# A Perceiver block in fp32: the first attention's value projection by seven products of matrix quarters, its bias behind the weighing, queries and the results' high parts through DRAM

## The reference

```
q = query @ Wq + bq                      # 16 x 64 x 1024, 16 heads of 64
k = key @ Wk + bk                        # 16 x 512 x 1024
v = value @ Wv + bv                      # 16 x 512 x 1024, key = value = ctx_1024
attn = softmax(einsum('bqhd,bkhd->bhqk', q, k) / 8)
out = einsum('bhqk,bkhd->bqhd', attn, v) @ Wo + bo + residual
```

## Time and profile before

| | us |
|---|---|
| median of the runs | 1711.32 |
| the profiled execution | 1711.51 |
| its span, first to last instruction | 1709.7 |
| PE busy | 1615.2 |
| DVE busy | 1163.9 |
| ACT busy | 938.0 |
| POOL busy | 307.3 |

### The profile page before, as it was taken

How to read it: one execution, slowest core, us unless ns; L and a number is a source line. 1 busy time by engine, 2 the same in 40 slices (tenths; PEclk the granted TensorE clock), 3 DMA queues, 4 the chain that set the end, 5 groups by cost and what they waited for, 6 DMA issues and landing times. The chain is left out here.

```text
span 1709.7 us, 27478 instructions
## 1 busy us (share of the span) xinstructions
PE 1615.2 (94%) x10730; PEld 1361.0 (80%) x10730; DVE 1163.9 (68%) x1978; ACT 938.0 (55%) x1700; POOL 307.3 (18%) x258
## 2 busy tenths in 40 slices
PE   7999999999999999999999878994899999999987
PEld 6888888888888888888887766773788888888876
DVE  4277777877777777777777666775768448548842
ACT  5466666666666666666666433442656336336631
POOL 4201211011101110111100161565311011101101
PEclk9999999999999999999999999996999999999899
DMA  6601830111101110111002560114757437528711
GB/s 228 212 24 54 131 77 7 54 57 54 37 27 53 57 54 8 54 56 54 7 5 80 173 187 14 55 57 138 249 150 212 141 87 242 155 89 247 221 39 21
DMA packets 54107, 165.21 MB, mean 97 GB/s; under 512 B 10612, under 2 KB 10996, under 8 KB 53408
## 3 DMA queue, kind: packets, MB, share of 16 engines
q1 hardware_dynamic: 38032, 131.88, 22.6%
q0 software_dynamic: 15920, 31.19, 8.7%
HBM read 143.54 MB, written 55.64 MB: 117 GB/s over the span
## 5 line engine op out<-in xcount | busy, mean ns | idle before, releaser
L413 PE MATMUL psum<-ctx,Wk 128*128 128x512 f32 x1536 | 386.2, 400 | 0.0
L413 PE MATMUL psum<-Wv,ctx 128*128 128x512 f32 x1536 | 368.7, 389 | 0.0
L413 PEld LDWEIGHTS psum<-Wv,ctx 128*128 128x128 f32 x1536 | 288.3, 188 | 59.9
L413 PEld LDWEIGHTS psum<-ctx,Wk 128*128 128x128 f32 x1536 | 280.1, 189 | 55.9
L932 DVE SCALAR_TENSOR_TENSOR kT<-psum,bkc,kT 64x512 fp32r<-64x512 f32 x256 | 191.9, 750 | 170.0 <-ACT kT L1322 165.8
L413 PE MATMUL psum<-xgT,Wh 128*128 128x224 f32 (+5 forms) x1536 | 250.0, 316 | 15.1 <-issue 10.2
L413 PEld LDWEIGHTS psum<-xgT,Wh 128*128 128x128 f32 x1536 | 228.4, 196 | 32.7 <-issue 12.6
L766 PE MATMUL psum<-Wh,hs 128*128 128x512 f32 x981 | 245.6, 396 | 0.0
L1332 ACT ACTIVATE Pr<-Pr,smn 128x512 f32<-128x512 f32 x128 | 92.6, 724 | 233.9 <-DVE smn L941 233.9
L1322 ACT ACTIVATE kT<-psum,bkc 64x512 fp32r<-64x512 f32 x256 | 175.1, 684 | 77.7 <-PE psum L413 73.8
L766 PEld LDWEIGHTS psum<-Wh,hs 128*128 128x128 f32 x981 | 181.1, 190 | 33.7 <-DVE hs L1207 0.3
(11 more groups left out here) (154 smaller groups left out, 1911.1 us busy)
## 6 DMA issues: line engine op xcount, KB each, us to landing
raw<-in_W SPq DMA_DIRECT2D x128, 512.0 KB, 4.3
expert_rows<-in_spare_rows SPq DMA_DIRECT2D x16, 1042.0 KB, 7.3
raw<-in_ctxT SPq DMA_DIRECT2D x32, 512.0 KB, 4.4
xg<-expert_rows POOLq DMA_DIRECT2D x32, 256.0 KB, 5.9
low_parts<-Olo POOLq DMA_DIRECT2D x32, 128.0 KB, 2.4
oT<-low_parts SPq DMA_DIRECT2D x8, 512.0 KB, 4.3
out_x<-x SPq DMA_DIRECT2D x12, 256.0 KB, 2.2
xs<-in_x SPq DMA_DIRECT2D x4, 512.0 KB, 6.8
```

Source lines behind the costliest of these rows:

```text
L413: mm = pe.matmul(dst, l, r, start=n == 0, stop=n == len(pairs) - 1)
```

## The change

**Seven products.** Context (512 keys by 512) and Wv (512 by 1024) are cut in quarters, A11 to A22 and B11 to B22. Four sums of context quarters (S1 to S4) and four of weight quarters (T1 to T4) are made, and the values come from seven quarter products, where eight tiles' worth of products stood: P1 = A11 B11, P2 = A12 B21, P3 = S4 B22, P4 = A22 T4, P5 = S1 T1, P6 = S2 T2, P7 = S3 T3. A product covers one tile of 128 keys and 512 dims and has 6 matmuls. For each batch there are two groups G = 2b + p of seven products (84 matmuls, 96 before). The order in the steps is fixed by `v_products(n)`: P1 and P6 in steps j = 2 and 6, P2 and P7 in j = 3 and 7, P4 and P5 in j = 4 and 0, P3 alone in j = 5 and 1. PE does `weigh` ahead of them now. `weigh` waits until both groups of its batch are done. Two PSUM banks serve the products in turn.

**Moving them out.** ACT copies P1 to a value tile (`move_v`); DVE adds the others to tiles, one addition each for P6, P2, P7, P4 and P3, and two for P5 (`evict_v`). That is 12 additions on DVE per batch for 8.

**Sums.** Per batch POOL makes four sums of 128x512 (`ctx_sums`) and four low parts (`sums_low`), ACT four high parts (`sums_high`, at the end of steps 4, 4, 6 and 7). For batch 0 DVE does POOL's part behind the last query product. The sums of weights are made once, on DVE and ACT, while queries are projected.

**Bias.** bv is added to the weighed result: `o_high` and `o_low` are now four instructions of 64 columns each, since the bias differs from head pair to head pair.

**DRAM.** Each query tile goes to `q_rows` in DRAM through a ring of four (`qst`, POOL's DMA) and comes back batch by batch (`qb`). The queries qs are built for half a batch at a time, in steps 2 and 6. The results' high parts go to `high_parts` beside the low ones, and SP fetches both before the output products.

**Elsewhere.** `d_gate(NT - 1)`, ACT's exponential in the routing of the last tile, stands ahead of the high part of the fourth expert weight tile. In the experts DVE's `weighted` waits for all chunks (`y_psum`) where it began at the first (`y_ready`), and POOL issues small DMAs for the missing chunks for every expert.

The diff, cut to its core:

```diff
+        V_ORDER = ("P1", "P6", "P2", "P7", "P4", "P5", "P3")
+        def v_bank(G, name):
+            return bank[2 + (7 * G + V_ORDER.index(name)) % 2]
+        def v_products(n):
+            if n < 2:
+                return ((0, "P1"), (0, "P6")) if n == 0 else ((0, "P2"), (0, "P7"), (0, "P4"), (0, "P5"))
+            G, names = {2: ((n + 2) // 4, ("P1", "P6")), 3: ((n + 1) // 4, ("P2", "P7")), 0: (n // 4, ("P4", "P5")), 1: ((n - 1) // 4, ("P3",))}[n % 4]
+            return (((0, "P3"),) if n == 2 else ()) + (tuple((G, name) for name in names) if G < NG else ())
...
@@ tensor_program: weigh
-                pe.wait_ge(v_done, HALF * (u + 1))
+                b, g = divmod(u, 2)
+                pe.wait_ge(v_done, 7 * (2 * b + 2))
...
-            for n in range(HALF):
-                project_v(n)
             for n in range(NS + 3):
                 if n < NS:
                     project_k(n)
                 if 0 <= n - 1 < NS:
                     scores(n - 1)
-                if n + HALF < NS:
-                    project_v(n + HALF)
                 if n >= 6 and n % HALF == 2:
                     weigh(n // HALF - 1)
+                for G, name in v_products(n):
+                    project_v(G, name)
                 if 0 <= n - 2 < NS:
                     turn(n - 2)
@@ vector_program
+            def evict_v(G, name):
+                n, src = 7 * G, v_bank(G, name)
+                v.wait_ge(v_psum, n + V_ORDER.index(name) + 1)
+                if name == "P6":
+                    v.wait_ge(v_moved, G + 1)
...
+                elif name == "P5":
+                    v.wait_ge(v_done, n + 4)
+                    v.tensor_tensor(v_tile(G, 1, 1), src, v_tile(G, 1, 1), ALU.add).then_inc(v_done, 1)
+                    v.tensor_tensor(v_tile(G, 0, 1), src, v_tile(G, 0, 1), ALU.add).then_inc(v_done, 1)
@@ scalar_program
+                for s_ in range(HALF):
+                    high = s.activation(Ohr[u % 4][:, s_, :], bank[7][:, s_ * TB:(s_ + 1) * TB], ACT.Identity,
+                                        bias=bvc[:, HALF * half + s_:HALF * half + s_ + 1])
...
-                if n < NS and j == 2 and b + 1 < B:
-                    build_qbd(b + 1)
+                for G, name in v_products(n):
+                    move_v(G, name)
+                if n % HALF == 2 and n // HALF + 1 < NS // HALF:
+                    build_qbd(n // HALF + 1)
...
+                if n < NS and b + 1 < B and j in (4, 6, 7):
+                    sums_high(b + 1, {4: ("S2", "S3"), 6: ("S1",), 7: ("S4",)}[j])
...
-            split_first(3)
             d_gate(NT - 1)
+            split_first(3)
@@ gpsimd_program
+            for n in range(2 * NJ):
+                g.wait_ge(q_done, n + 1)
+                g.dma_start(q_rows[n // NJ, n % NJ], qst[n % 4][:]).then_inc(q_out[n % 4], 16)
...
+                if b < B:
+                    ctx_sums(b)
...
+                    sums_low(b)
```

More of the change, by code:

```diff
@@ L243, in perceiver_block @@
         y_psum, y_ready, y_done, out_added, scattered = (sem(n) for n in ("y_psum", "y_ready", "y_done", "out_added", "scattered"))
-        out_wide = [sem(f"out_wide{q}") for q in range(2 * E)]
+        out_wide = sem("out_wide")
         LAG = 3
@@ L299, in sync_program, with fetch_qb @@
             fetch_ctx(0)
[L300 to L304, removed]
+            for k in range(KD):
+                fetch(L_WK + k, a["Wk"][k * P:(k + 1) * P, :])
+            for m, k in enumerate(VK):
+                fetch(L_WV + m, a["Wv"][k * P:(k + 1) * P, :])
+            for c in range(2):
+                fetch(sum_load(0, c), a["ctxT"][0, :, 2 * c:2 * c + 2, :])
+            def fetch_qb(b):
+                half, at = divmod(b, 8)
+                if b < 2:
+                    for r in range(4):
+                        sp.wait_ge(q_out[r], 64 if r <= b else 32)
+                else:
+                    sp.wait_ge(qbd_hi, 8 * (b - 1))
+                    sp.wait_ge(qbd_lo, 4 * (b - 1))
+                if b == 8:
+                    for r in range(4):
+                        sp.wait_ge(q_out[r], 64)
+                sp.dma_start(qb[b % 2][:], q_rows[half, :, :, at * TB:(at + 1) * TB].rearrange("j p t -> p j t")).then_inc(qb_in[b % 2], 16)
+            fetch_qb(0)
+            fetch_qb(1)
             for b in range(B):
@@ L472, in tensor_program, with key_tile @@
                 project_q(n, slice(n // NJ * 512, n // NJ * 512 + 512), True)
[L474 to L488, removed]
-                else:
-                    pe.wait_ge(v_done, n - 1)
-                products(v_bank(n), split_pairs([pair(ctx[b % 2], slice(None), k, ks) for k in range(KD)],
-                                                      [pair(Wv, slice(None), k, cs) for k in range(KD)])).then_inc(v_psum, 1)
+            def key_tile(x, p):
+                return [[x[i][:, kk, p * P:(p + 1) * P] for i in range(2)] for kk in range(2)]
@@ L553, in c_product @@
                     pe.wait_ge(o_lo, NS // HALF)
-                products(c_bank(t), split_pairs([(Ohi[:, j, rows], oT[t % 4][:, j, :]) for j in range(NJ)],
+                products(c_bank(t), split_pairs([(oH[t][:, j, :] if t < 2 else Ohi[:, j, rows], oT[t % 4][:, j, :]) for j in range(NJ)],
                                                   [pair(Wo, slice(None), j) for j in range(NJ)])).then_inc(c_psum, 1)
-            for n in range(HALF):
-                project_v(n)
             for n in range(NS + 3):
@@ L911, in o_low @@
             def o_low(u):
-                b, half = divmod(u, 2)
-                hi = Ohi[:, HALF * half:HALF * (half + 1), b * TB:(b + 1) * TB]
+                half = u % 2
                 v.wait_ge(o_hi, u + 1)
@@ L917, in o_low @@
                 else:
-                    v.wait_ge(low_out[u % 4], 16 * (u // 4))
-                v.tensor_tensor(Olo[u % 4][:], bank[7][:, 0:HALF * TB].rearrange("p (s q) -> p s q", s=HALF), hi, ALU.subtract).then_inc(o_lo, 1)
+                    v.wait_ge(low_out[u % 4], 32 * (u // 4))
+                for s_ in range(HALF):
+                    low = v.scalar_tensor_tensor(Olo[u % 4][:, s_, :], bank[7][:, s_ * TB:(s_ + 1) * TB], bvc[:, HALF * half + s_:HALF * half + s_ + 1],
+                                                 Ohr[u % 4][:, s_, :], ALU.add, ALU.subtract)
+                low.then_inc(o_lo, 1)
             v.wait_ge(qbd_zero, 4)
             build_qbd(0)
-            for n in range(HALF):
-                evict_v(n)
             for n in range(NS + 1):
```

397 lines of the change are left out of this document (298 added, 99 removed).

## The result

The changed kernel takes 1757.84 us (median of 4 runs, 1754.28 to 1760.32) against 1711.26 (1709.48 to 1712.38) in the same comparison: ratio 1.0272, 95% interval 1.0251 to 1.0293. The forecast was 1741 with a range of 1714 to 1768. The profiled execution of after has a span of 1758.4 us, 48.7 more than before.

What follows compares the result with a forecast made beforehand. PE bounded the loop before; after the change the ring of ACT and DVE would. 1711.5 plus 21 (ring), 5 (port), 4 (startup), 2 (end), minus 2 (routing) gave 1741.5, forecast as 1741 us, range 1714 to 1768.

Steps and rivals of the forecast that it cites:

- What bounds the kernel, and the margin of 5.5 us: Attention loop before: PE needs 55.4 us a block, the ring of ACT and DVE 49.9, leaving 5.5.
- PE's saving of 44 us is real, and it turns into waits: Attention loop: 12 matmuls fewer a batch save PE 2.73 us, times 16, but PE then waits.
- The short step can't be used in full: Loop steps j = 1 and 5: six value matmuls need PE 5.0 us, less than the 5.63 of ACT and DVE.
- the walk: Step-by-step reckoning of one changed block, 56.7 us against 55.4, and of the startup, K(3) at 96.0 for 92.3.
- The ring, +1.4 a block: Loop: ACT and DVE's fixed order with the new work takes 56.7 us a block against 55.4; +21 in all.
- The port, +0.3 a block: Loop: DVE's scaling waits beside POOL's work, a quarter of the 1.2 us bound a block; +5, at most +18.
- rival 4: Loop: DVE waits in full for POOL's instructions by the skill's rule; +13 over the sum, 1754 us; chance 0.10.
- rival 3: Loop: PE's clock falls to the 1.2 GHz level behind its waits; 21 us more, 1762 us; chance 0.17.
- Startup, +4: Start of attention: K(3) at 96.0 us for 92.3, first scores near 78; bounds 0 and +10.
- End of the loop and output products, +2: Last steps: three moves and four-part copies add about 1.5, the high parts' DMA 0 to 4; taken as +2.
- Routing, -2: Last tile: DVE's 2.67 us wait for ACT's exponential goes, POOL's send is late next; bounds 0 and -2.7.
- Experts, 0: Experts: DVE begins to weigh up to 1 us later for seven experts; 0, up to +5.

Runs made afterwards that it cites:

- experiment 5: Kernel before, with ScalarE's copy of the turned weights made twice in every step: 1711.89 us, ratio 1.0006, a block 55.21 us.
- experiment 6: Same second ScalarE copy, in the kernel before with 12 value matmuls fewer a block: 1713.24 us, ratio 1.0019, a block 54.88 instead of 52.49.
- experiment 4: Kernel before, with one value product in four made of 6 matmuls instead of 12: 1675.02 us, ratio 0.9808, a block 52.49 us.
- experiment 3: Changed kernel with GpSimd's eight operations a block on sums and low parts cut to 8 columns of 512: a block 56.35 us, whole time (2508 us) unusable.
- experiment 10: Reordered changed kernel of 1677.99 us, with half of the second attention's key weights loaded ahead of the last results' fetches: 1678.05 us, ratio 0.9800.
- experiments 7 and 8: First: changed kernel, ScalarE's work moved into its waits and P1 a step earlier, 1688.45 us. Second: that kernel with the attention's start reordered, 1684.19 us.

## Why the prediction came out as it did

- **What bounds the kernel, and the margin of 5.5 us:** right. 5 us of ScalarE work fit under PE (experiment 5), and the sum 8 x 5.63 + 4.9 with 0.62 more a step met the measured block within 0.1 us, and the blocks in the middle of the loop within 0.2 (experiment 6).
- **"PE's saving of 44 us is real, and it turns into waits":** right. Alone it is worth 2.74 us a block (experiment 4; reckoned 2.73), and the change got none of it.
- **"The short step can't be used in full":** wrong as reckoned. In experiment 4 it was used in full. The floor of 5.63 holds for the sum over steps that can lend to each other. In the changed kernel the short step lies in a ring that is over PE anyway, so by the walk the error had no effect on the sum; no run tests that.
- **The ring, +1.4 a block:** measured 56.35 - 55.23 = 1.1 without collisions (experiment 3). The new instructions' prices held: copies of 64x256 414 ns (0.42), the four high parts 0.80 to the next start (1.0), a sum's high 0.52 (0.53). Step j = 2 took 8.66 (8.8), j = 6 9.18 (9.3), and j = 0 and 1 together 12.3 (12.1).
- **The port, +0.3 a block:** mis-sized; 0.96. The walk saw two meetings, at the sum S4 and at the low parts of step 4, and then took a quarter of the bound. A third, in step 1, isn't in it (0.75 us for 0.49). The prediction's own sign of rival 4, scalings above 0.49 while POOL is busy, was there. The rule of the Trainium skill (SBUF — State Buffer, Who interferes with whom), by which the two-port scaling waits for a whole GpSimd instruction, agrees with this trace: 1.57 and 1.29 us instead of 0.49, each ending 0.3 us after POOL's instruction. The prediction's upper bound, 1.2 a block, was near.
- **The clock:** rival 3 did not come. The granted clock was 1.00 in the stage 200 to 400 with all those waits.
- **Startup, +4:** the term that was furthest off, 13.0, and outside its own bounds of 0 and 10. Three steps of the walk failed. First, it kept the end of the query products at 63.87, and they ended at 67.92. PE began the last 96 of them 2.4 us later, since DVE's part of x stood behind ACT's copy of a weight tile, which waited 6.96 us for its load (5.24 before). Then they took 1.6 us longer. Before, and after:

```profile
42.02 22.01 PE L413 MATMUL psum<-xnT,Wq 128*128 128x512 f32 x96 [0.41 <-DVE xnT L866]
```

```profile
44.43 23.65 PE L507 MATMUL psum<-xnT,Wq 128*128 128x512 f32 x96 [2.13 <-DVE xnT L982]
```

  Second, it had DVE's sums begin at 63.87. The sums of the weights kept DVE busy until 67.5, and then it waited 4.24 us for a load; P6 waited for the sums, with K(1) behind it. The first `scores` came at 86.53, where the prediction had 78 and called anything after 82 a sign of being wrong (DVE's timeline, then PE's):

```profile
71.76 0.69 DVE L1040 TENSOR_TENSOR tS<-raw,raw 128x512 f32<-128x512 f32 x1 [4.24 <-DMA raw<-in_ctxT]
```

```profile
75.50 2.54 PE L507 MATMUL psum<-T,S 128*128 128x512 f32 x6 [3.34 <-DVE S L1051]
77.83 3.63 PE L507 MATMUL psum<-ctx,Wk 128*128 128x512 f32 x12
86.53 1.19 PE L637 MATMUL psum<-kT,qs 128*128 128x512 f32 x2 [5.07 <-DVE kT L1111]
87.52 2.53 PE L507 MATMUL psum<-B,ctx 128*128 128x512 f32 x6
...
102.56 2.27 PE L507 MATMUL psum<-T,S 128*128 128x512 f32 x6 [2.15 <-DVE V L1088]
```

  Third, it priced waits and not what follows them: after each, six matmuls took 2.3 to 2.5 us where 1.52 is usual. The granted clock (third column from the end) is down to 0.50, the 1.2 GHz level, in stretches shortly behind the waits of 2.13 and 2.15 us:

```profile
46.00:48.00 2.00, 2.00 (x6) 1.61 (x5) 1.69 (x2) 0.00 (x0) 0.00 (x0) 0.50 0.78 195
104.00:106.00 2.00, 2.00 (x8) 1.61 (x8) 1.04 (x3) 0.90 (x3) 1.02 (x1) 0.50 0.00 0
```

- **End of the loop and output products, +2:** measured +0.3 and +5.1. The wait behind the stores of the last results was not in the walk; whether the +5.1 comes from it is open (experiment 10).
- **Routing, -2:** -3.0 between the routing's last matmul and the first expert rows; DVE's wait of 2.67 us for the exponential is down to 0.17. **Experts, 0:** +2.2, less than the 3.7 by which the same expert code differs between experiments 7 and 8. That and the +1.5 in the second attention weren't tried.

The direction and what bounds the loop were right for the reasons given. The time lies in the range, but above the forecast's own 1752, next to the prices of rivals 3 (which did not happen) and 4 (which mostly did). That it lies in the range at all is partly luck: the startup missed by 9 us with no rival for it, and in the loop a ring term too large covered part of a port term too small. The profiled execution took 1760.3 us, 18.8 over the sum: 9 from the startup, 3 from the end and the output products, some 4 in the loop (port 9 to 10 too small, ring 4 to 5 too large), 3 from the stages behind.

## What to carry to other kernels

When one engine is full and the others wait in a fixed order, reckon the next ring before you lighten the full one, as a sum over the steps that can lend to each other. Work that is added to the waiting engines is free only up to that margin, and it counts by its place: put it where that engine waits in the ring (here 1.8 us ahead of each exponential) and not behind. If a saving turns into waits, the cure may be the order alone: here the same instructions went from 1757.8 to 1678.0 us.

## What the runs showed of the hardware

- A scaling of 128x512 on DVE that meets a POOL sum or low part ends some 0.3 us after it: 0.75, 1.57 and 1.29 us for 0.49. VectorE's moves out of PSUM of the same shape stayed at 681 to 693 ns with POOL busy 35% of the time.
- Waits of PE of 0.7 to 1.2 us several times in a block left the granted clock at 1.00; behind the waits of 2.1 to 5.1 us between 42 and 103 us stretches of 2 us stood at 0.50 to 0.65.
- A second copy on ACT that waits for the end of the first puts 0.62 us on a step, where one that follows without a wait takes 0.48 to the next start (448.15 to 448.63 in experiment 4's kernel).
